# An attention and expert block: turned halves and split weights carried into the shared tiles; first rows loaded beside the constants, stacks cleared behind the first rows

## The chip, the cores and the metric

The kernel runs on one core of one Trainium2 chip. The core has a matrix engine (TensorE, PE in the rows), VectorE (DVE), ScalarE (ACT), GpSimd (POOL) and SyncE (SP), which here only issues DMA transfers. Each engine works through its own instructions in order and waits on semaphores that others raise. The metric is the time of one execution in microseconds (us); lower is better.

## The reference, cut to what matters

Two layers run over 8 sequences of 512 tokens of width 256, 4096 tokens in all.

```python
qkv = einsum('bsd,hde->bhse', x, Wqkv) + bqkv          # layer 0 attention, 16 heads of 16, causal
x = x + softmax(q @ k.T / 4) @ v @ Wout + bout         # with a layer norm before it
h = silu((xf @ w1 + b1) * (xf @ w3 + b3))              # layer 0 experts: 352 hidden units
y = sum over the 2 chosen of 8 experts of rw * (h @ w2 + b2)
z = shared expert, same form, on every token           # y + z is added to x
...                                                    # layer 1: gated scan, latent experts
```

Products in f32 are made of three products in f16: each operand is split into a high half and a low half (value minus high half), and high x high, low x high and high x low are summed.

## The kernel before, in words

Three phases follow each other, each a block that ends with a barrier over all engines.

**Mix phase** (`mix_phase`): for each sequence b the normalised rows xn are turned (transposed) on PE, split by ACT (`x_high`) and DVE (`x_low`) into `xT_hi` and `xT_lo`, and give q, k, v and the router's logits. q and k go through DRAM into `q_stack` and `k_stack` (`store_hi`, `load_stacks` on SP). The heads follow, three steps a head (`at = 3*head + n`), and the preparation of the next sequences hangs on these steps by tables (`AT_X_T`, `AT_Q`, ...). xn is also stored to DRAM, as rows. A small block before it, `constants`, makes identity matrices on POOL while the others wait. The mix block begins with nine loads on SP, a clearing of `q_stack` on DVE and one of `k_stack` on POOL. It ends when SP has seen the last store of x1 (the residual) land.

**Experts phase** (`experts_phase`): tiles of 256 tokens. The shared expert takes 16 of them: tiles 0 to 10 first (`HEAD` and, the last two, `TURN`), then the routed tiles, 8 experts with at least two tiles each, then the last five shared ones (stages 0 to 4). A tile is, on PE: `gate_up` for m = 0 and 1, the four transposes that turn the rows of the next tile (`x_transposes`), `gate_up` for m = 2, then `out` of the tile before. Each `gate_up` is 12 products of 256 columns, `out` is 18. ACT and DVE split the turned rows (`x_part`), add biases, gate (`prod`), apply silu (`h`, `h_hi`, `h_lo`) and sum the output (`y`). `gate_up` of a tile waits for the `prod` of the tile before. In the first tiles DVE also does `place`, which writes one-hot columns (`in_column`), 7 a tile, and a split of later weights (`pack_lo`); POOL writes 64 one-hot rows (`in_lane`), then 8 columns and 2 more. After tile 8 PE multiplies all of them (`table`) into the list of tokens that POOL then gathers by.

Before tile 0 the phase loads the shared expert's weights and the first rows, turns the rows and splits both; `find_slots` on DVE works out the slots from the router's results, and only then can DVE do anything for tile 0.

**Layer 1** (`layer1_phase`) begins when the last shared tile is done; its first normalisation hangs on gathered rows that DVE adds in stages 2 and 3.

## Time and profile before

| what | us |
|---|---|
| three runs: lowest, median, highest | 1232.79, 1236.97, 1238.09 |
| the profiled execution | 1237.58 |
| its span, first to last instruction | 1235.8 |
| PE busy | 1124.0 |
| DVE busy | 914.1 |
| ACT busy | 682.2 |
| POOL busy | 529.9 |

The shares are averages over phases: the mix phase takes the first 463 us, the experts phase runs to about 845, layer 1 to the end. Where two rows of one engine stand back to back, a change matters if it removes one of them; where a row shows idle time with a releaser, the releaser sets the time.

### The profile page before, as it was taken

The numbers are of one execution on the slowest core, as the hardware profiler recorded it, in microseconds if no ns is written. First come the engines' busy times: TensorE is split into PE (matmuls) and PEld (weight loads), VectorE is DVE, ScalarE is ACT, GpSimd is POOL, SyncE is SP. The second block draws the span as 40 slices with busy tenths as digits, with TensorE's granted clock in tenths as the row PEclk, the third lists the DMA queues.
The fourth block names the chain that finished last, engine by engine and source line by source line (L and its number), as shares of the span: only waits on it lengthen the run. The fifth ranks groups of instructions, "written<-read, shape, count | busy, mean of one in ns | idle before, by whom it ended". The sixth has DMA issues, their size and how long they took to land. (4 is left out here: it accounts for less than half of the span.)

```text
span 1235.8 us, 26934 instructions
## 1 busy us (share of the span) xinstructions
PE 1124.0 (91%) x8964; PEld 751.5 (61%) x8965; DVE 914.1 (74%) x2224; ACT 682.2 (55%) x1478; POOL 529.9 (43%) x751
## 2 busy tenths in 40 slices
PE   4789999999999966998999999997999999999998
PEld 2345555555555435887999888883555555546555
DVE  4778898888887826885756667674877977977866
ACT  2256565665556544665656666655554654664553
POOL 5343333424333228833444443332635546447314
PEclk9689999999999997999999999998999999999999
DMA  4437524445234106656232453442231241332302
GB/s 137 82 72 215 108 45 95 95 78 102 45 79 87 18 35 190 192 161 197 76 126 81 123 163 122 121 141 69 81 126 41 97 129 42 102 94 72 107 8 97
DMA packets 98276, 125.17 MB, mean 101 GB/s; under 512 B 14480, under 2 KB 87888, under 8 KB 97168
## 3 DMA queue, kind: packets, MB, share of 16 engines
q1 hardware_dynamic: 87184, 105.07, 31.9%
q0 software_dynamic: 6912, 18.88, 5.5%
q8 instruction: 47, 0.77, 0.3%
q10 hardware_dynamic: 4096, 0.14, 0.2%
q14 instruction: 37, 0.30, 0.1%
HBM read 84.70 MB, written 39.19 MB: 100 GB/s over the span
## 5 line engine op out<-in xcount | busy, mean ns | idle before, releaser
L479 ACT ACTIVATE p<-bank 128x384 f32<-128x384 f32 (+1 forms) x384 | 191.5, 530 | 186.0 <-PE bank L855 119.6
L688 DVE TENSOR_REDUCE neg_max<-bank 128x1 f16<-128x384 f32 (+3 forms) x352 | 219.6, 640 | 65.0 <-PE bank L843 62.2
L397 POOL TENSOR_SCALAR_AFFINE_SELECT p<-p 128x256 f32<-128x256 f32 x256 | 103.6, 409 | 245.4 <-ACT p L479 244.7
L121 PE MATMUL xbank<-gT_hi,w_hi 128*128 128x256 f16 (+1 forms) x636 | 175.0, 275 | 15.3 <-DVE w_lo L1448 6.0
L122 PE MATMUL xbank<-gT_lo,w_hi 128*128 128x256 f16 (+1 forms) x636 | 174.7, 275 | 0.0
L123 PE MATMUL xbank<-gT_hi,w_lo 128*128 128x256 f16 (+1 forms) x636 | 174.6, 274 | 0.0
L840 PE MATMUL bank<-k_stack,q_stack 96*128 96x384 f16 (+3 forms) x512 | 133.5, 313 | 20.1 <-DVE neg_max L688 12.6
L1382 ACT ACTIVATE a<-xbank,b 128x256 f32<-128x256 f32 x159 | 74.3, 468 | 65.9 <-PE xbank L123 62.4
L1293 POOL DMA_INDIRECT fetched<-xn_dram,token_now x80 | 81.4, 1017 | 42.9 <-POOL token_now L1289 30.7
L1934 POOL TENSOR_TENSOR up_lo<-up_sq,up_hi 128x512 f16<-128x512 f32 x32 | 43.2, 1378 | 126.6 <-ACT up_hi L1991 126.6
L1467 DVE SCALAR_TENSOR_TENSOR prod<-xbank,b,a 128x256 f32<-128x256 f32 x159 | 73.8, 476 | 31.4 <-ACT a L1382 23.7
L855 PE MATMUL bank<-q_stack,k_stack 97*128 97x512 f16 (+1 forms) x256 | 91.1, 360 | 3.8 <-ACT p L479 3.8
L1945 POOL TENSOR_TENSOR he_lo<-he_sq,he_hi 128x512 f16<-128x512 f32 x64 | 75.6, 1200 | 43.4 <-ACT he_hi L2032 43.4
L121 PE MATMUL xbank<-w_hi,h_hi 128*128 128x256 f16 (+1 forms) x318 | 88.1, 277 | 5.4 <-DVE y L1482 5.4
L843 PE MATMUL bank<-mask_qk,identb 128*128 128x128 bf16 (+2 forms) x352 | 89.1, 253 | 0.0
L122 PE MATMUL xbank<-w_lo,h_hi 128*128 128x256 f16 (+1 forms) x318 | 87.9, 277 | 0.0
L123 PE MATMUL xbank<-w_hi,h_lo 128*128 128x256 f16 (+1 forms) x318 | 87.9, 276 | 0.0
L2032 ACT ACTIVATE he_hi<-he_sq 128x512 f16<-128x512 f32 x64 | 39.4, 627 | 85.0 <-DVE he_sq L2169 85.0
L873 PE MATMUL bank<-p,v_aug 128*32 128x512 f32 (+3 forms) x1024 | 83.1, 443 | 0.8 <-DVE o_rows L668 0.8
L1473 DVE TENSOR_TENSOR h_lo<-h,h_hi 128x256 f16<-128x256 f32 x159 | 66.9, 425 | 22.6 <-ACT h_hi L1391 21.9
L121 PEld LDWEIGHTS xbank<-gT_hi,w_hi 128*128 128x128 f16 (+1 forms) x636 | 67.9, 107 | 25.1 <-issue 12.1
L840 PEld LDWEIGHTS bank<-k_stack,q_stack 96*128 96x128 f16 x512 | 45.0, 99 | 59.0 <-DVE neg_max L688 41.1
(304 smaller groups left out, 3065.5 us busy)
## 6 DMA issues: line engine op xcount, KB each, us to landing
w_bc<-wT_dram SPq DMA_DIRECT2D x8, 2048.0 KB, 8.3
y_routed_dram<-y SPq DMA_DIRECT2D x37, 256.0 KB, 2.1
w<-in_w SPq DMA_DIRECT2D x11, 704.0 KB, 6.8
pack<-in_pack SPq DMA_DIRECT2D x12, 342.0 KB, 4.0
xr<-in_x SPq DMA_DIRECT2D x8, 512.0 KB, 7.3
xn_dram<-xn SPq DMA_DIRECT2D x8, 512.0 KB, 3.1
qk_hi_dram<-qk_hi SPq DMA_DIRECT2D x16, 256.0 KB, 2.8
qk_lo_dram<-qk_lo SPq DMA_DIRECT2D x16, 256.0 KB, 2.6
```

Of the source, the lines that this page charges most:

```text
L121: pe.matmul(out, hi_a(c), hi_b(c), start=first and x == 0, stop=False)
L122: pe.matmul(out, hi_a(c), lo_b(c), start=False, stop=False)
L123: mm = pe.matmul(out, lo_a(c), hi_b(c), start=False, stop=last and x == n - 1)
L397: pool.affine_select(out=diagonal, in_=diagonal, pattern=[[0, 2], [1, P]], compare_op=ALU.is_ge, fill=0.0, base=0, channel_multiplier=-1). ...
L479: act.activation(p32[:, s // GH % 2, s % GH, cols], s_bank[n][:, 0:cols.stop - cols.start], ACT.Exp).then_inc(p_exp.sem, 1)
L688: dve.tensor_reduce(neg_max[:, g % 2, 0:GH * TT].rearrange("p (h t) -> p h t", t=TT)[:, heads[0]:heads[-1] + 1, j], a_bank[c % 2][:, 0:len ...
L840: pe.matmul(to[:, at * w:(at + 1) * w], q_stack[0:STK, u, h0 + h, j * P:(j + 1) * P], k_stack[0:STK, u, h0 + h, 0:w], start=at == 0, stop= ...
L843: pe.matmul(diagonal, identb[:, :], mask_qk[:, 0:len(heads), :], start=False, stop=True).then_inc(a_psum.sem, 1)
L855: mm = pe.matmul(to[:, 0:S - n * P], k_stack[0:AUG, u, h, n * P:(n + 1) * P], q_stack[0:AUG, u, h, n * P:S], start=True, stop=True)
L873: mm = pe.matmul(out_bank[VW * h:VW * (h + 1), k * P:S], v_aug[:, b % 2, k, GH * (g % NG) + h, :], p32[:, g % 2, h, P_OFF[k]:P_OFF[k] + S ...
L1293: pool.indirect_dma_start(fetched[:, u, half, :], None, dram["xn"], bass.IndirectOffsetOnAxis(token_now[:, u, half:half + 1], 0)).then_inc ...
L1945: pool.tensor_tensor(he_lo[:, e, :], he_sq[:, e % EB, :], he_hi[:, e, :], ALU.subtract).then_inc(he_lo_s.sem, 1)
```

## The change

1. **First loads.** The loads of x for sequence 0 and of wqkv are issued by SP inside the `constants` block. The clearing of `q_stack` and of `k_stack` moves behind the work on the first rows.
2. **Turned halves.** In the mix phase SP stores `xT_hi` and `xT_lo` of every sequence to DRAM (`store_xT`, 2 x 256 KB each). The shared tiles, all but tile 11 (stage 0), load them ready split into one of two `turned` tiles; their transposes and `x_part` go away. Tile 11 and the routed tiles keep theirs.
3. **Split weights.** The shared expert's weights are loaded and split in the last sequence of the mix phase, into tiles that outlive it (`Carried`). Biases come from there too. The loads of expert 1's and 2's weights move by a tile or two.
4. **Barrier.** The mix block no longer waits for the last store of x1; the load that needs it does.
5. **Columns.** DVE places 8 columns in each of tiles 0 to 7 (64 in all), POOL none of these.

```diff
-AHEAD = 2
-PLACED_BY_DVE = 56
-PLACED_A_TILE = 7
+PLACED_BY_DVE = 64
+PLACED_A_TILE = 8
+AT_SHARED = (3, 5, 8, 10)
+class Carried:
...
+        self.first = sb("shared_in", [P, 2 * DC * 3 * D], F16)
+        self.second = sb("shared_out", [P, 2 * len(HT) * D], F16)
+        self.turned = sb("turned", [P, 2, 2, DC, ETOK], F16)
+        self.bias = sb("shared_b13", [P, 2 * len(HT)])
...
 # mix phase, SP
-            sp.dma_start(xr[:, :, :], rows(x, 0)).then_inc(x_loaded.sem, 16)
-            sp.dma_start(wqkv32[:, :, :], w["wqkv"].rearrange("(c p) n -> p c n", p=P)).then_inc(wqkv_loaded.sem, 16)
...
+            def store_xT(b):
+                sp.wait_ge(xT_lo_s.sem, xT_lo_s.at(b))
+                for k, of in enumerate((xT_hi, xT_lo)):
+                    sp.dma_start(dram["xnT"][b][:, k], of[:, :, :]).then_inc(xT_stored.sem, 16)
...
             store_xn(0)
             load_x(1)
+            store_xT(0)
...
+                if b + 1 == NB:
+                    sp.wait_ge(xT_stored.sem, xT_stored.at(0))
+                    load_shared()
...
-            sp.wait_ge(x1_stored.sem, x1_stored.at(NB - 1))
+            sp.wait_ge(x1_stored.sem, x1_stored.at(NB - 2))
+            sp.wait_ge(xT_stored.sem, xT_stored.at(NB - 1))
 # mix phase, POOL
-            clear(k_stack, 0)
...
             inverse_std(0)
+            clear(k_stack, 0)
 # mix phase, ACT (and the like on DVE, two steps later, into the low halves)
+            def split_shared(n):
...
+                if n < 2:
+                    act.activation(carried.w13_hi[:, n, :], w13_32[n], ACT.Copy).then_inc(w_hi.sem, 1)
+                elif n == 2:
+                    act.activation(carried.w2_hi[:, 0:2, :], w2_32[:, 0:2, :], ACT.Copy).then_inc(w_hi.sem, 1)
...
+                    elif at - 28 in AT_SHARED:
+                        split_shared(AT_SHARED.index(at - 28))
 # constants
+        @block.sync
+        def _(sp):
+            sp.dma_start(carried.xr[:, :, :], w["x"][0:S, :].rearrange("(t p) d -> p t d", p=P)).then_inc(carried.x_loaded.sem, 16)
+            sp.dma_start(carried.wqkv32, w["wqkv"].rearrange("(c p) n -> p c n", p=P)).then_inc(carried.wqkv_loaded.sem, 16)
 # experts phase, SP
+            def load_turned(n, tile, read):
+
+                sp.wait_ge(gu_psum.sem, gu_psum.at(read))
+                sp.dma_start(turned[:, n % 2], turned_tile(dram["xnT"], tile)).then_inc(turned_loaded[n % 2].sem, 16)
...
-                if stage == HEAD:
-                    load_x(i + AHEAD)
                 load_pack(i)
+                load_turned(i + 2, i + 2 + (i + 2) // HEAD_TILES, i)
...
             def prologue():
-                load_x(0)
-                load_weights(0, 0)
                 load_biases(0, 0)
-                load_x(1)
 # experts phase, ACT (the same on DVE, after find_slots)
             def prologue():
                 act.activation(identh[:, :], identf[:, :], ACT.Copy).then_inc(identh_s.sem, 1)
-                x_part(0)
-                for c in range(DC):
-                    split_in(0, 0, c, 0)
-                split_out(0, 0, 0)
...
-                if has_next(stage):
+                if next_routed(i, stage):
                     x_part(i + 1)
 # experts phase, PE
-                pe.wait_ge(gT_lo_s.sem, gT_lo_s.at(i))
-                gate_up(i, u, 0)
-                gate_up(i, u, 1)
-                if has_next(stage):
-                    x_transposes(i + 1, stage == HEAD or is_int(i, HEAD_TILES - AHEAD), stage + 1 if stage in range(TAIL_TILES) else 0)
-                gate_up(i, u, 2)
+                n = shared_place(i, stage)
+                if n is None:
+                    pe.wait_ge(gT_lo_s.sem, gT_lo_s.at(i - HEAD_TILES))
+                else:
+                    pe.wait_ge(turned_loaded[n % 2].sem, turned_loaded[n % 2].at(n // 2))
+                gate_up(i, u, 0, n)
+                gate_up(i, u, 1, n)
+                if next_routed(i, stage):
+                    x_transposes(i + 1)
+                gate_up(i, u, 2, n)
```

DVE at the start of the mix phase, before (line numbers are the source's; xr holds the rows of x, xn the normalised ones):

```order
L535 UNCONDITIONAL_BRANCH [waits barrier_Pool_Activation_PE_DVE_SP_release]
L539 MEMSET q_stack 96x4096
L542 MEMSET route_run 128x8
L543 MEMSET neg_max 128x32
L549 BN_STATS stats<-xr 128x6 [waits x_loaded,cleared]
```

And of the change, from the split of the gate's weights to the low halves of k:

```order
L784 TENSOR_SCALAR bq<-bqk 128x2 [waits w_loaded]
L786 TENSOR_TENSOR gate_lo<-gate,gate_hi 128x16 [waits w_hi]
L788 TENSOR_TENSOR wout_lo<-shared_out,wout_hi 128x512 [waits w_hi]
L608 MEMSET q_stack 96x4096
L646 SCALAR_TENSOR_TENSOR qk_lo<-bank,bqk,qk_hi 128x512 [waits qk_hi_s] x2
```

The clearing of `q_stack` moved from ahead of the first statistics to ahead of the first low half of k.

PE where the experts phase begins, before (xg holds a tile's rows, gT_hi and gT_lo the turned halves, w_hi and w_lo the weights' halves):

```order
L1624 UNCONDITIONAL_BRANCH [waits barrier_Pool_Activation_PE_DVE_SP_release]
L1636 MATMUL xbank<-identf,xg 128x128 [waits tile_loaded]
L1636 MATMUL xbank<-identf,xg 128x128 x3
L121 MATMUL xbank<-gT_hi,w_hi 128x256 [waits e_lo,prod_s,gT_lo_s]
L122 MATMUL xbank<-gT_lo,w_hi 128x256
```

And of the change (the weights' halves stand in shared_in):

```order
L1695 UNCONDITIONAL_BRANCH [waits barrier_Pool_Activation_PE_DVE_SP_release]
L149 MATMUL xbank<-turned,shared_in 128x256 [waits prod_s,turned_loaded0]
L150 MATMUL xbank<-turned,shared_in 128x256
L151 MATMUL xbank<-turned,shared_in 128x256
L149 MATMUL xbank<-turned,shared_in 128x256
```

The first product follows the barrier with no transposes, no load and no split in between.

DVE from the end of `find_slots` through tile 0 to tile 1, of the change:

```order
L1675 CAST lanes_half<-lanes 128x128 [waits slots]
L1614 COPY slot<-pos 128x8
L1615 COPY wk<-route_weights 128x8
L1541 SCALAR_TENSOR_TENSOR prod<-xbank,shared_b,a 128x256 [waits h_hi_s,a1_s,b_loaded]
L1541 SCALAR_TENSOR_TENSOR prod<-xbank,shared_b,a 128x256 [waits h_hi_s,a1_s]
L1541 SCALAR_TENSOR_TENSOR prod<-xbank,shared_b,a 96x256 [waits h_hi_s,a1_s]
L1547 TENSOR_TENSOR h_lo<-h,h_hi 128x256 [waits h_hi_s] x2
L1547 TENSOR_TENSOR h_lo<-h,h_hi 96x256 [waits h_hi_s]
L1609 TENSOR_SCALAR in_column<-lanes_half,pos_f,ids 128x114 [waits lanes_half_s]
L1609 TENSOR_SCALAR in_column<-lanes_half,pos_f,ids 128x114 x7
```

Before, five rows stood between the copy of `wk` and the first `prod`: one `gT_lo` and four splits of weights; `find_slots` itself has not moved.

## Rows read from the trace of the kernel before

**Rows 1.** Windows, a shared tile's stretch: PE, PEld, DVE, ACT, POOL busy, clock, DMA
```profile
507.10:513.46 6.36, 6.36 (x61) 5.87 (x60) 6.09 (x18) 4.29 (x11) 6.36 (x9) 1.00 0.59 182
```

**Rows 2.** Timeline, the start: start, us, engine, line, operation, idle before
```profile
0.79 0.53 POOL L981 MEMSET zeros<- 128x512 f32 x1 [0.29 <-POOLq L2436]
...
2.54 0.65 POOL L996 TENSOR_SCALAR_AFFINE_SELECT mask_qk<-zeros 128x512 bf16<-128x512 f32 x1
...
3.66 0.45 SPq L274 DMA_DIRECT2D xr<-in_x  x1
...
4.59 3.47 DVE L539 MEMSET q_stack<- 96x4096 f32 x1 [4.46 <-PEq L972]
...
8.15 1.41 DVE L549 BATCH_NORM_STATS2 stats<-xr 128x6 f32<-128x256 f32 x4
...
12.84 0.21 ACT L437 ACTIVATE gate_hi<-gate 128x16 f16<-128x16 f32 x1 [1.74 <-DMA shared_b_row<-in_b]
...
22.12 0.75 DVE L578 SCALAR_TENSOR_TENSOR qk_lo<-bank,bqk,qk_hi 128x512 f16<-128x512 f32 x1 [5.07 <-ACT qk_hi L461]
```

**Rows 3.** Timeline, ACT in the last sequence's heads
```profile
441.16 1.36 ACT L479 ACTIVATE p<-bank 128x512 f32<-128x512 f32 x3 [0.50 <-PE bank L855]
...
442.87 2.80 ACT L479 ACTIVATE p<-bank 128x512 f32<-128x512 f32 x6
```

**Rows 4.** Timeline, the end of the mix phase to tile 1
```profile
460.30 0.38 SPq L294 DMA_DIRECT2D x_dram<-x  x1
...
463.56 0.82 SPq L1220 DMA_DIRECT2D xg<-xn_dram  x2
...
469.35 0.16 DVE L1540 COPY wk<-route_weights 128x8 f32<-128x8 f32 x1
...
470.28 1.47 ACT L1363 ACTIVATE w_hi<-w 128x704 f16<-128x704 f32 x2 [2.43 <-DMA w<-in_w]
...
473.24 0.37 PE L121 MATMUL xbank<-gT_hi,w_hi 128*128 128x256 f16 x1 [6.01 <-DVE w_lo L1448]
...
481.67 0.28 PE L121 MATMUL xbank<-gT_hi,w_hi 128*128 128x256 f16 x1 [1.48 <-DVE gT_lo L1460]
```

**Rows 5.** Windows, the first products of tile 0
```profile
473.00:476.00 3.00, 2.76 (x14) 1.98 (x15) 1.01 (x2) 0.00 (x0) 3.00 (x5) 0.50 0.00 0
```

**Rows 6.** Timeline, PE: one tile's transposes and the product behind
```profile
490.66 0.60 PE L1636 MATMUL xbank<-identf,xg 128*128 128x128 f32 x4
...
491.10 0.27 PE L121 MATMUL xbank<-gT_hi,w_hi 128*96 128x256 f16 x1
```

**Rows 7.** Timeline, PE: transposes of later tiles
```profile
499.42 0.66 PE L1636 MATMUL xbank<-identf,xg 128*128 128x128 f32 x4 [2.25 <-DMA xg<-xn_dram]
...
512.14 0.60 PE L1636 MATMUL xbank<-identf,xg 128*128 128x128 f32 x4
518.48 0.60 PE L1636 MATMUL xbank<-identf,xg 128*128 128x128 f32 x4
```

**Rows 8.** Timeline, DVE in a shared tile
```profile
505.31 1.76 DVE L1534 TENSOR_SCALAR in_column<-lanes_half,pos_f,ids 128x114 f16<-128x114 f16 x7
...
508.54 0.67 DVE L1460 TENSOR_TENSOR gT_lo<-xbank,gT_hi 128x512 f16<-128x512 f32 x1
```

**Rows 9.** Tile in_lane: ns min/median/max, first and last start
```profile
L1320 POOL TENSOR_SCALAR in_lane<-lanes,pos_f x64: 592/604/1713, 469.3 to 512.2; 128x128 f16<-128x128 f32 x64
```

**Rows 10.** Timeline, POOL's last column and PE's table
```profile
519.68 2.32 POOL L1328 TENSOR_SCALAR in_column<-lanes,tail_at,tail_ids 128x114 f16<-128x114 f32 x2
...
535.01 3.48 PE L1699 MATMUL xbank<-in_column,in_lane 128*128 128x114 f16 x64
```

**Rows 11.** Tile xg: landing of a tile's rows after issue
```profile
DMA to landing us min/median/max: 2.0/3.1/6.1
```

**Rows 12.** Timeline, the last shared tiles
```profile
808.47 0.28 PE L121 MATMUL xbank<-gT_hi,w_hi 128*128 128x256 f16 x1 [1.05 <-DVE gT_lo L1460]
...
829.58 0.99 DVE L1549 SCALAR_TENSOR_TENSOR x<-rows_k,wk,x 128x256 f32<-128x256 f32 x2
```

More of the change, by code:

```diff
@@ L341, in _ @@
                 if b + 1 < NB:
+                    store_xT(b + 1)
                     store_hi(b + 1, 0)
@@ L494, in out_copy @@
                 act.activation(o_cols[:, g % 2, :], out_bank[:, :], ACT.Copy).then_inc(o_copied.sem, 1)
+            def split_shared(n):
+                loads = shared_in_loaded if n < 2 else shared_out_loaded
+                act.wait_ge(loads.sem, loads.at(0))
+                if n < 2:
[3 more added lines that the diff above has]
+                else:
+                    act.activation(carried.w2_hi[0:HT[2][1], 2, :], w2_32[0:HT[2][1], 2, :], ACT.Copy).then_inc(w_hi.sem, 1)
             for c in range(DC):
@@ L1106, in experts_phase @@
         rows_moved = sig("rows_moved", 1)
-        x_loaded = sig("tile_loaded", 16 * HALF)
-        tail_loaded = [sig(f"tail_loaded{t}", 16) for t in range(1, TAIL_TILES)]
+        turned, turned_loaded = carried.turned, carried.turned_loaded
         gT_psum = sig("gT_psum", 1)
@@ L1142, in over_experts @@
             tile(1, 0, 0, HEAD)
-            for i in range(2, HEAD_TILES - AHEAD):
+            for i in range(2, HEAD_TILES - 2):
                 tile(i, 0, 0, HEAD)
@@ L1258, in tile @@
                     load_pack(PACK_PARTS - 1)
-                    for t in range(1, TAIL_TILES):
-                        rows = dram["xn"][(HEAD_TILES + t) * ETOK:(HEAD_TILES + t + 1) * ETOK, :]
-                        sp.dma_start(tail_rows[:, t - 1, :, :], rows.rearrange("(h p) d -> p h d", p=P)).then_inc(tail_loaded[t - 1].sem, 16)
             def last(e, u, first):
@@ L1321, in _ @@
             ins.then_inc(lane_placed.sem, 1)
-            for t in range(PLACED_BY_DVE // 2, T // P):
-                for k in range(2):
-                    ins = pool.tensor_scalar(in_column[:, 2 * t + k, :], lanes[:, 0:columns], pos_f[:, 0, t, k:k + 1],
-                                             ids[:, t:t + 1], ALU.is_equal, ALU.mult)
-            ins.then_inc(column_placed.sem, 1)
             for k in range(TAIL_PLACES):
@@ L1604, in prologue @@
                 find_slots()
-                x_part(0)
-                for c in range(DC):
-                    split_in(0, 0, c, 0)
-                split_out(0, 0, 0)
             def after_first(e, u, first):
@@ L1636, in x_transposes, with gate_up @@
                         mm = pe.transpose(bank[3][:, c * ETOK + half * P:c * ETOK + half * P + P],
-                                          rows[:, half, c * P:(c + 1) * P], identf[:, :])
+                                          xg[:, half, c * P:(c + 1) * P], identf[:, :])
                 mm.then_inc(gT_psum.sem, 1)
-            def gate_up(i, u, m):
+            def gate_up(i, u, m, n):
                 h0, M = HT[m]
+                x_hi, x_lo = (xT_hi, xT_lo) if n is None else (turned[:, n % 2, 0], turned[:, n % 2, 1])
                 pe.wait_ge(prod_s.sem, prod_s.at(i - 1, m + 1))
@@ L1705, in after_first @@
                 if not is_int(e, 0):
-                    pe.wait_ge(e_lo.sem, e_lo.at(e))
+                    pe.wait_ge(e_lo.sem, e_lo.at(e - 1))
                     pe.nop(nofuse=True)
-            over_experts(pe, lambda: x_transposes(0, True), new_expert, tile, after_first, lambda e, u, first: None, table, out)
+            over_experts(pe, lambda: None, new_expert, tile, after_first, lambda e, u, first: None, table, out)
 PACK = {}
```

208 lines of the change are left out of this document (126 added, 82 removed).

## The prediction

> **What bounds the kernel now.** I read the windows first, then the timeline at each place that the diff touches, then single tiles. In a shared tile PE has no gap, 6.36 us of 6.36, and DVE is busy for 6.09 of them, POOL for all; the clock is 1.00, its 2.4 GHz level [rows 1]. So PE bounds these tiles and DVE stands close behind. Two tiles' transposes stand 6.34 apart (512.14 and 518.48), which is the period of a tile [rows 7]. Between the phases nothing bounds but a chain: x1 is stored at 460.30, the next phase's first load is issued at 463.56, weights arrive for ACT at 470.28, the first product starts at 473.24 after 6.01 idle, and tile 1 at 481.67 [rows 4]. That chain is where most of the change acts.
>
> **1. Start.** x is issued at 3.66, and its statistics start at 8.15, right behind a clearing of `q_stack` that runs from 4.59 to 8.06 [rows 2]. So x had landed within 4.5 us of its issue at the latest. SP will now issue it where the first operation of `constants` stands, at about 0.8 [rows 2]: landed by 5.3, and DVE is free from about 4.8. The gain is 2.85 to 3.35, say 3.1. The last of the nine small loads reaches ACT at 12.84 [rows 2]; ACT must split the gate's and the output's weights from it before the turned rows. It was issued at about 7.7, 5.1 earlier. Now it is the eighth behind two that went ahead, issued at 7.2, and takes between 2.0, the shortest landing of a tile's rows [rows 11], and the same 5.1. ACT then turns to the rows at 10.0 to 13.1, where everything else is ready at 11.0 (14.1 less 3.1). The middle, 11.6, gives 2.5 of gain. Against it, `store_xT(0)` puts 512 KB between the next x and the stores of q and k, all on one queue: 0 to 1.4, I take 0.5. The moved clearing (3.47 us) is hidden: DVE had 5.07 idle before the first low half of k at 22.12 [rows 2], which now comes near 19.6, and the clearing starts near 14. The one on POOL (as long, estimated) falls into POOL's wait for the turned rows. If that cover were gone it would cost the overhang. **Start: -2.0 (-3.4 to -0.5).**
>
> **2. Mix phase.** Seven more pairs of stores go to SP between waits that end later anyway (q and k are products of the very halves that are stored), so nothing queues behind them. In the last sequence ACT gets four splits. Two of 704 columns took 1.47 together [rows 4]; the two for w2 (768 columns) are estimated from it at 0.9: 2.4 in all. There ACT runs its exponentials with little room: 0.50 idle before 441.16, then 2.80 in one piece [rows 3]. At most 2.4 - 0.5 = 1.9 reaches the end of the phase, at least nothing (PE has work of its own between). I take 1.0. DVE, which mirrors the splits, has no maxima left by then. **+1.0 (0 to +1.9).**
>
> **3. Between the phases.** The landing of x1 is no longer waited for. What is left is the issue (460.30 + 0.38) and a barrier; the one after `constants` took 0.47 (POOL's end at 3.19, first issue at 3.66) [rows 2, 4]. The phase begins at about 461.2 instead of 463.56. The `turned` halves and weights are there, so PE does tile 0 (36 products, about 3.9 us by 0.109 each) at once. Then it waits: `find_slots` ends 5.95 after the phase's first issue (469.51 less 463.56) [rows 4], and it has not moved. So DVE is free at 467.15, the first `prod` takes some 0.45, and tile 1 starts at 467.6 instead of 481.67. **DVE is late next**; behind `find_slots` are queued `prod`, the low halves and the columns, and PE waits for them. Before, tile 0 ran at clock 0.50, the 1.2 GHz level, after 6.01 idle [rows 4, 5]; the pause is now about 2 us, and I take full clock.
>
> **4. Shared tiles 1 to 8.** Four transposes cost 491.10 - 490.66 = 0.44 [rows 6]. A tile is then 6.34 - 0.44 = 5.90. DVE loses `gT_lo` and gains a column: seven take 1.76, one 0.25, and `gT_lo` takes 0.60 of its queue (0.67 less overlap) [rows 8]: 6.09 - 0.60 + 0.25 = 5.74, just under. The wait of 2.25 for a tile's rows [rows 7] goes. The table can start at 467.6 + 8 x 5.90 = 514.8. It also needs POOL. POOL starts `in_lane` at 469.3, 5.74 after the phase's first issue, and now at 466.95. Its 64 rows took 43.5 (469.3 to 512.2 and one more), against 64 x 0.604 = 38.7 by the median; the longest took 1.713 [rows 9]. Five bursts of DVE's columns lay in that time, so a burst of seven cost POOL 0.96. Eight bursts of eight cost 8.8: 466.95 + 38.7 + 8.8 = 514.4, and two columns of at least 0.8 make 516.0. Some of the excess may have other causes, so I take 515.5. Before, POOL ended at 522.0 and PE began at 535.01 [rows 10]: the 13 us of cover are gone. **Places 3 and 4 together: 535.0 - 515.5 = -19.5 (-20.2 to -17.5).**
>
> The Trainium skill (SBUF — State Buffer, Who interferes with whom) speaks against this: VectorE and GpSimd share a port pair as an "exclusive lock", and a 16-bit `tensor_scalar` can hold it for its whole length. By that rule every column stops POOL fully. The trace bears it out by half: a burst of 1.76 cost 0.96.
>
> **5. Tile 9** loses its transposes, tile 10 keeps them for tile 11: **-0.44**. The gather of the first routed rows shifts with the table.
>
> **6. Last shared tiles.** Stage 1 started at 808.47, after 1.05 idle for `gT_lo` [rows 12]. It will wait for `prod` instead, which DVE does just before. Stages 0 to 3 lose 0.44 each: at most 1.05 + 1.76 = 2.8. But layer 1 hangs on gathered rows that DVE adds from 829.58 [rows 12], and POOL's gathers start only when the last routed tile's y has landed, which moves by `gT_lo` alone, 0.6. I take 2.0. **-2.0 (-2.8 to -0.6).**
>
> **Sum.** -2.0 + 1.0 - 19.5 - 0.44 - 2.0 = -22.9. The profiled execution took 1237.58, which is 0.6 above the median of the three runs; so 1214.6 in its terms, 1214.0 beside the median. The routed tiles and layer 1 have the same work as before.
>
> **Rivals.**
> - *POOL is locked out in full.* DVE's eight bursts of 8 x 0.25 all add to POOL's 38.7: 466.95 + 38.7 + 16.1 + 1.2 = 523. The table waits 7.5 longer than forecast: 1221.5. For it: POOL's 1.713 us row. Against it: five bursts would have made 47.5 where 43.5 stood [rows 9]. 12 in 100. (That is the skill's rule of the exclusive lock taken whole.)
> - *Start and splits pay nothing back.* The small loads land as late as before and the ACT splits reach PE in full, the tail gives 0.6: -0.5 + 1.9 - 19.5 - 0.44 - 0.6 = -19.1, 1218. For it: the exponentials' solid 2.80 [rows 3]. 17 in 100.
> - *More than forecast.* Every term at its good end: -26.8, 1210; 6 in 100.
> - *The change doesn't do what it says*: the clock stays at its lower level through tile 0 and 1 (1.4 + 5.9 lost), and DVE bounds the tiles at 6.3, 3 more: 1224 to 1232. Against it: the short pause. 5 in 100.
> - *Slower.* The `turned` loads come late. One can be issued when tile i has done its `gate_up`, 3.9 into it, and is needed 11.8 after the tile's start: 7.9 of room. xg took 3.1 at the median and 6.1 at most [rows 11]. Thirteen loads must each be 1.8 over the room to eat 22.9, which means 9.7 to land; at 10.0 the time is 1214 + 13 x 2.1 = 1241. The pieces are half as long (512 bytes), which speaks for slower landing, but not threefold. 2 in 100.
> - The forecast (1210.5 to 1217.5): 58 in 100.
>
> **The numbers.** 1214.0. The range 1209 to 1222 takes in the first three rivals nearly whole, some 85 in 100 with the scatter of runs. A measurement of this kernel can tell about 0.5%, 6.2 us, from no change. All but the last two cases lie below 1230.8: faster 0.94, same 0.04, slower 0.02.
>
> **What would show it.** In the changed profile: statistics of x at about 5; PE's first product of the experts phase near 460 (461.2 less the start and split terms) at clock 1.00; one idle stretch of about 2.5 behind it, released by `prod`; then tiles 5.90 apart with no transposes; the table near 514.5 (515.5 less the same), released by POOL or by nothing; POOL's last column within 2 us of it. Wrong would be: tiles over 6.1 apart, waits for `turned` halves, a table released by POOL after 518, a mix phase longer than before by over 2, or a clock of 0.50 behind the barrier.

## The result

The changed kernel takes 1229.54 us (median of 8 runs, 1227.47 to 1233.48), the kernel before 1236.84 (8 runs, 1231.95 to 1243.53): ratio 0.9948, 95% interval 0.9925 to 0.997. Run again beside other kernels it took 1229.95, ratio 0.9946 (0.9923 to 0.9969). It is faster, by 7 us or 0.5%, which is clear of the scatter; forecast were 23, and a range of 1209 to 1222. The profiled execution took 1229.52, its span 1227.8, against 1237.58 and 1235.8 before.

The rows that answer to those of before follow in the order of the prediction's steps. **Start** (timeline of the changed kernel; start, us, engine, line, operation, idle before and what ended it):

```profile
4.64 1.41 DVE L617 BATCH_NORM_STATS2 stats<-xr 128x6 f32<-128x256 f32 x4 [0.78 <-DMA xr<-in_x]
8.08 4.48 DVE L635 TENSOR_SCALAR xn<-xr,mv,rstd 128x256 f32<-128x256 f32 x4 [1.56 <-issue]
...
7.93 3.51 POOL L427 MEMSET k_stack<- 96x4096 f32 x1
...
20.16 0.51 SPq L326 DMA_DIRECT2D xnT_dram<-xT_hi  x1
20.71 0.43 SPq L326 DMA_DIRECT2D xnT_dram<-xT_lo  x1
...
26.68 0.33 SPq L376 DMA_DIRECT2D q_stack<-qk_hi_dram  x1
...
32.12 0.58 PE L921 MATMUL bank<-k_stack,q_stack 96*128 96x128 f16 x4 [4.93 <-DMA k_stack<-qk_hi_dram]
```

The statistics start at 4.64, 3.5 earlier than in [rows 2]; forecast were 2.85 to 3.35. Then everything is given back: the normalising takes 4.48 us (1.38 before) just while POOL clears `k_stack`, so that it ends 0.35 earlier than before (12.56 for 12.91), and two more stores stand in front of q and k. The first product of scores comes at 32.12; before it came at 30.71.

**Phase border** (timelines of SP and PE, then windows with PE, PEld, DVE, ACT, POOL busy, clock, DMA share, GB/s):

```profile
462.80 0.37 SPq L345 DMA_DIRECT2D x_dram<-x  x1
463.76 0.36 SPq L1275 DMA_DIRECT2D b<-in_b  x1
...
464.10 0.27 PE L149 MATMUL xbank<-turned,shared_in 128*128 128x256 f16 x1 [2.13 <-PEq L161]
470.25 0.27 PE L149 MATMUL xbank<-turned,shared_in 128*128 128x256 f16 x1 [0.40 <-DVE prod L1541]
477.06 0.27 PE L149 MATMUL xbank<-turned,shared_in 128*128 128x256 f16 x1 [0.75 <-DVE prod L1541]
...
483.62 0.27 PE L149 MATMUL xbank<-turned,shared_in 128*128 128x256 f16 x1 [0.50 <-DVE prod L1541]
494.79 0.40 PE L149 MATMUL xbank<-turned,shared_in 128*128 128x256 f16 x1 [5.11 <-DMA turned<-xnT_dram]
...
527.13 3.47 PE L1769 MATMUL xbank<-in_column,in_lane 128*128 128x114 f16 x64 [0.56 <-DVE prod L1541]
```

```profile
462.00:464.00 2.00, 0.00 (x0) 0.00 (x0) 0.69 (x1) 0.22 (x1) 0.22 (x2) 1.00 0.13 46
464.00:466.00 2.00, 1.90 (x14) 1.55 (x15) 1.27 (x7) 0.09 (x1) 0.52 (x8) 0.76 0.89 266
466.00:468.00 2.00, 2.00 (x11) 1.45 (x10) 1.84 (x6) 0.47 (x1) 0.00 (x0) 0.50 0.88 255
...
492.00:494.00 2.00, 0.00 (x0) 0.00 (x0) 0.41 (x1) 0.00 (x0) 2.00 (x4) 0.59 0.43 140
494.00:496.00 2.00, 1.21 (x6) 0.89 (x7) 0.44 (x2) 0.77 (x1) 2.00 (x5) 0.50 0.56 101
```

x1's last store is issued at 462.80, 2.5 later than in [rows 4]; the border takes 0.96 (forecast 0.9), PE is at work 0.34 behind it, and tile 1 starts 6.49 after the phase's first issue (forecast 6.4). But the clock falls to its 1.2 GHz level in tile 0 (0.50 from 465.0 to 468.5). Tile 2 starts 6.81 after tile 1, tile 3 another 6.56 later, both released by `prod`, and then tile 4 waits 5.11 for its turned halves and starts at half clock.

SP, in front of that wait (timeline):

```profile
474.37 0.53 SPq L1308 DMA_DIRECT2D turned<-xnT_dram  x1
480.12 0.40 SPq L1312 DMA_DIRECT2D y_dram<-y  x1
...
481.61 0.91 SPq L1281 DMA_DIRECT2D b<-in_b  x2
482.56 0.44 SPq L1269 DMA_DIRECT2D w<-in_w  x1
...
483.56 2.20 SPq L1271 DMA_DIRECT2D w<-in_w  x1
485.80 0.63 SPq L1318 DMA_DIRECT2D pack<-in_pack  x1
486.47 0.68 SPq L1308 DMA_DIRECT2D turned<-xnT_dram  x1
```

Tile 2 had done its `gate_up` near 481 (477.06 + 3.9). The buffer was free then; the load that fills it is issued at 486.47, behind y(0) and the whole of expert 1. It lands 8.3 us later, the longest of the 13 in this phase (median 4.2; xg had 3.1 and at most 6.1, [rows 11]).

DVE in the same tiles and in a later one (timeline), the window of one round, then POOL's rows (the tile's line with ns min/median/max, and single rows from the timelines: two of the changed kernel, one of the kernel before):

```profile
483.00 1.25 DVE L1541 SCALAR_TENSOR_TENSOR prod<-xbank,shared_b,a 128x256 f32<-128x256 f32 x3
...
485.49 0.42 DVE L1547 TENSOR_TENSOR h_lo<-h,h_hi 96x256 f16<-96x256 f32 x1 [0.17 <-ACT h_hi L1468]
485.83 0.74 DVE L1556 TENSOR_TENSOR y<-xbank,xr 128x256 f32<-128x256 f32 x2
486.49 2.33 DVE L1609 TENSOR_SCALAR in_column<-lanes_half,pos_f,ids 128x114 f16<-128x114 f16 x8
488.72 0.86 DVE L1602 TENSOR_TENSOR pack_lo<-pack,pack_hi 128x684 f16<-128x684 f32 x1
489.50 1.26 DVE L1541 SCALAR_TENSOR_TENSOR prod<-xbank,shared_b,a 128x256 f32<-128x256 f32 x3
...
517.17 1.84 DVE L1609 TENSOR_SCALAR in_column<-lanes_half,pos_f,ids 128x114 f16<-128x114 f16 x8
```

```profile
483.00:489.50 6.50, 6.00 (x56) 5.34 (x54) 6.20 (x18) 3.87 (x10) 6.50 (x11) 1.00 0.76 202
```

```profile
L1402 POOL TENSOR_SCALAR in_lane<-lanes,pos_f x64: 590/596/1652, 469.5 to 509.2; 128x128 f16<-128x128 f32 x64
...
487.02 0.59 POOL L1402 TENSOR_SCALAR in_lane<-lanes,pos_f 128x128 f16<-128x128 f32 x1
488.75 1.30 POOL L1402 TENSOR_SCALAR in_lane<-lanes,pos_f 128x128 f16<-128x128 f32 x1
...
497.65 1.66 POOL L1320 TENSOR_SCALAR in_lane<-lanes,pos_f 128x128 f16<-128x128 f32 x1
```

While POOL works, one round of DVE is 6.50 (483.00 to 489.50) with no idle but 0.17 and 6.20 of it busy: DVE bounds. Eight columns take 2.33 there and 1.84 once POOL is done. POOL's 64 rows take 40.3 in all. The row at 487.02, beside columns, takes 0.59; the one at 488.75, beside `pack_lo`, takes 1.30. Rows follow each other 0.58 apart otherwise, which makes 37.1 for 64. Of the other 3.2, 3.0 stand in four places beside `pack_lo` and 0.2 beside columns.

The last shared tiles (timelines of SP and PE, windows):

```profile
806.97 0.38 SPq L1312 DMA_DIRECT2D y_dram<-y  x1
...
808.01 0.59 SPq L1308 DMA_DIRECT2D turned<-xnT_dram  x1
...
798.31 0.28 PE L149 MATMUL xbank<-turned,w_hi 128*128 128x256 f16 x1 [0.46 <-DVE prod L1541]
...
812.85 0.28 PE L149 MATMUL xbank<-turned,w_hi 128*128 128x256 f16 x1 [2.05 <-DMA turned<-xnT_dram]
```

```profile
815.00:820.00 5.00, 5.00 (x41) 4.29 (x40) 1.90 (x5) 2.05 (x5) 0.95 (x1) 0.84 0.53 175
```

Stage 1 starts at 798.31 instead of 808.47 [rows 12]; its buffer is free at 802.2, and the next load is issued at 808.01, behind the store of stage 0. Stage 3 waits 2.05 and runs in part at the lower clock.

### The profile page after: what moved, and what is told of

Its sections match the earlier page's. It is cut to its first block and busy times, and to the rows that moved or that the text cites. A ratio compares the mean times of both kernels' runs of the same rounds, so it can differ in the third digit from the quotient of the medians.

```text
span 1227.8 us, 26691 instructions
## 1 busy us (share of the span) xinstructions
PE 1118.7 (91%) x8873; PEld 747.1 (61%) x8905; DVE 915.4 (75%) x2217; ACT 676.3 (55%) x1463; POOL 520.6 (42%) x743
## 5 line engine op out<-in xcount | busy, mean ns | idle before, releaser
L1459 ACT ACTIVATE a<-xbank,b 128x256 f32<-128x256 f32 (+1 forms) x126 | 58.7, 469 | 55.1 <-PE xbank L151 51.5
L149 PE MATMUL ybank<-l_xT_hi,pack_hi 128*128 128x512 f16 x208 | 79.4, 382 | 0.9 <-DVE lat_lo L2251 0.7
L151 PE MATMUL ybank<-l_xT_hi,pack_lo 128*128 128x512 f16 x208 | 79.4, 382 | 0.0
L150 PE MATMUL ybank<-l_xT_lo,pack_hi 128*128 128x512 f16 x208 | 79.3, 381 | 0.0
L1541 DVE SCALAR_TENSOR_TENSOR prod<-xbank,b,a 128x256 f32<-128x256 f32 (+1 forms) x126 | 58.6, 477 | 25.9 <-ACT a L1459 22.9
L924 PE MATMUL bank<-mask_qk,identb 128*128 128x128 bf16 (+1 forms) x321 | 76.9, 240 | 0.0
L1466 ACT ACTIVATE h<-prod 128x256 f32<-128x256 f32 x159 | 64.9, 408 | 20.7 <-DVE prod L1541 13.5
L151 PE MATMUL ybank<-pack_hi,up_lo 128*128 128x256 f16 x256 | 69.8, 273 | 0.0
L150 PE MATMUL ybank<-pack_lo,up_hi 128*128 128x256 f16 x256 | 69.8, 273 | 0.0
L149 PE MATMUL ybank<-pack_hi,up_hi 128*128 128x256 f16 x256 | 69.8, 272 | 0.0
```

What stands on the lines that cost most here:

```text
L149: pe.matmul(out, hi_a(c), hi_b(c), start=first and x == 0, stop=False)
L150: pe.matmul(out, hi_a(c), lo_b(c), start=False, stop=False)
L151: mm = pe.matmul(out, lo_a(c), hi_b(c), start=False, stop=last and x == n - 1)
L924: pe.matmul(diagonal, identb[:, :], mask_qk[:, 0:len(heads), :], start=False, stop=True).then_inc(a_psum.sem, 1)
```

## The experiments

Each is the changed kernel with one edit, unless said otherwise. The expectations stand as they were recorded. Below them, a table with the readings of every profile.

**Weights behind turned halves.** SP, in `tile`:

```diff
                 load_turned(i + 2, i + 2 + (i + 2) // HEAD_TILES, i)
+                if is_int(i, 1): ... load_biases(1, 1); load_weights(1, 1)
+                if is_int(i, 3): ... load_weights(2, 0)
                 if before is not None:
                     store(i - 1, dram["y"], i - 1)
...
-                if is_int(i, 1): ...
-                if is_int(i, 3): ...
```

> The changed kernel with one move on SP's queue: in a shared tile the loads of expert 1 (tile 1) and expert 2 (tile 3) are issued right behind that tile's load of turned halves, ahead of the store of y, instead of behind it. Theory A (order in SP's queue): tile 4 waited 5.1 us because its halves were issued at 486.5, behind the store of y(0) at 480.1 and 5.2 us of issues for expert 1; now they are issued near 481 and tile 4 does not wait, the clock stays at 1.00 from tile 1 on, tiles stand 6.5 apart while POOL still works (DVE's columns at 0.30 each) and 5.92 after it, the table starts at 521.4 instead of 527.1, and the whole takes 1223.8 instead of 1229.5. Rival B (the transfers): the halves share the DMA engines with 1.1 MB of weights, so some tile between 2 and 5 still waits 3 us or more for its halves; table at 525 or later, whole 1227.5 or more.

Measured 1224.8 us. No tile up to the table waits for halves, and the table starts 59.16 after the phase's first issue instead of 63.37: 4.2 less, of 5.7 expected. Most of that goes with the clock, which stayed at 1.00 here in tile 0: two profiles below that have the changed kernel's order of loads and that clock start the table at 60.27 and 60.32, so the order by itself is worth 1.1 in these profiles. What it saves at tile 4 came back as a wait, in DVE's timeline:

```profile
487.50 0.76 DVE L1556 TENSOR_TENSOR y<-xbank,xr 128x256 f32<-128x256 f32 x2 [2.77 <-DMA y_dram<-y]
```

The store of y(0), now issued behind the weights, landed only there. So A holds for the halves, and B in a form of its own: what stands behind 1.1 MB pays.

**Last tiles' halves first.**

```diff
-                    if 1 <= stage and stage + 2 < TAIL_TILES:
-                        load_turned(HEAD_TILES + stage + 1, HEAD_TILES + stage + 2, i)
+                    if stage + 3 < TAIL_TILES:
+                        load_turned(HEAD_TILES + stage + 2, HEAD_TILES + stage + 3, i + 1)
                     store(i, dram["y"], HEAD_TILES + stage)
```

> The changed kernel with one move in the last shared tiles: the halves of stage s+3 are loaded as soon as stage s+1 has done its first products, ahead of the store of stage s. Theory A (order in SP's queue): the load for stage 3 was issued at 808.0 though its buffer was free at 802.2; now it is issued there, the wait of 2.05 us at 812.85 and the stretch at half clock behind it (about 2 us) go, and the end of the experts phase (first issue of layer 1, 838.6) comes 3 to 4 us earlier: 1226. Rival B: the end of the phase hangs on the gathered rows of the routed tiles and on DVE, so under 1 us comes back: 1229.

1224.96 us. No wait for halves, clock 1.00 up to 830.6 (28.6 into these tiles; in the changed kernel it falls at 813.2, 14.9 into them), and 36.87 from stage 1 to the phase's end where the changed kernel has 40.31. A holds.

**Clearing behind the normalising.**

```diff
             inverse_std(0)
+            pool.wait_ge(xn_ready.sem, xn_ready.at(0))
             clear(k_stack, 0)
```

> The changed kernel with POOL's clearing of k_stack made to wait until DVE has normalised the first rows. Theory A (DVE and POOL share a way to the buffer): the four normalising operations take 1.4 us instead of 4.48 and end at 9.5 instead of 12.56; ACT's first turned rows still wait for the small loads (gate_hi at 11.9) and come at 12.65 instead of 13.76: 1.1 us at the start. The next operation of DVE beside the clearing, wqkv_lo (1.75 us), may be stretched in turn. Whole 1228.4 instead of 1229.5. Rival B: the normalising is slow for another reason (late rows or a late reciprocal): it stays at 4.5 us.

1224.45 us. Its timeline:

```profile
8.28 1.38 DVE L636 TENSOR_SCALAR xn<-xr,mv,rstd 128x256 f32<-128x256 f32 x4 [1.56 <-issue]
9.57 1.75 DVE L781 TENSOR_TENSOR wqkv_lo<-shared_in,wqkv_hi 128x1536 f16<-128x1536 f32 x1
...
9.72 3.51 POOL L427 MEMSET k_stack<- 96x4096 f32 x1 [1.54 <-DVE xn L636]
```

The normalising is back at 1.38, so A holds. The same clearing does nothing to the subtraction beside it (1.75, as before). The gain at the first scores is 2.0 (30.18), more than the 1.1 expected: the first turned rows come 1.6 earlier (12.14 for 13.76), and PE's products for q and k stand 0.43 apart until 17.1 here and until 21.2 in the changed kernel, and 0.22 apart behind that, though the granted clock reads 1.00 throughout. What ends the slow stretch is open.

**Without the splits.** (`elif at - 28 in AT_SHARED: split_shared(...)` and its like on DVE removed, two memsets on POOL. It leaves out the shared expert's weights and computes with zeros.)

> The changed kernel without the splitting of the shared weights on ACT and DVE in the last sequence (left out: the shared expert is computed from zeros that POOL writes; loads as before). Theory A (ACT is on the path there): the changed kernel lost 1.4 us before 436 and 1.1 us more between 436 and the last store of x1 (462.80); without the splits that store comes at 461.7, and the whole takes 1228.4. Rival B (the splits are free and the lateness is all from the start): the last store stays at 462.8 within 0.2.

1225.56 us. From the output copy near 434 to the last store of x1: 26.36, exactly that of the kernel before, so the 1.1 of this stretch is the splits'. A holds for it. The store itself comes at 460.36, not 461.7: the part from the first scores to that copy is 1.5 shorter than in the changed kernel, which the edit does not touch. Over all profiles that part scatters between 401.4 and 404.2.

**Splits early.** `AT_SHARED = (3, 5, 8, 10)` becomes `(-6, -3, 0, 3)`.

> The changed kernel with the four splits of the shared weights moved from steps 31, 33, 36 and 38 of the last sequence to steps 22, 25, 28 and 31, where ACT still has idle time between its exponentials (2.5 to 3.6 us busy of every 5). Measured so far: from the output copy near 434 to the last store of x1 the kernel before takes 26.36 us, the one without splits 26.36, and the four profiles with splits 27.47, 28.83, 30.71 and 30.73. Theory A (the splits stand in ACT's solid stretch, and PE behind it sometimes falls to half clock): this stretch is 26.4 to 27 again, and the time from the first product of scores to the last store of x1 is 428 to 430.5; whole 1.1 to 4 us less than the changed kernel. Rival B (2.75 us of ACT work is paid wherever it stands): first scores to last store stays at 431 or more.

1224.94 us; 26.44 for the stretch, 428.65 from first scores to last store. The copy ahead of the stretch comes 13.55 behind the one before it, where the kernel before has 12.93: the splits now cost 0.6 there. A holds in this profile; of the four later ones with the same places one has 26.44 again and three have 28.02 to 29.69.

**Turned rows stored later.**

```diff
-            store_xT(0)
             for half in range(2):
                 store_hi(0, half)
                 load_stacks(0, half)
+                if half == 0:
+                    store_xT(0)
```

> The changed kernel with the two stores of the first batch's turned rows (512 KB) issued behind the first half's stacks instead of in front of the stores of q and k. Theory A (the low half of q and k lands late because it queues behind them): the first load into the stacks is issued at about 25.3 instead of 26.7 and the first product of scores comes at 30.7 instead of 32.1 to 32.3 (four profiles): whole 1.4 us less. Rival B (the landing is slow for the sake of the next x load, which was there before, too): first scores at 32 again.

1225.52 us; the first load into the stacks is issued at 25.23, and the first scores come at 30.86. A holds: 1.3.

**Columns 7 and 8, with the weights moved.** `PLACED_BY_DVE = 56`, `PLACED_A_TILE = 7`, and POOL's eight columns as before.

> The kernel with the expert weights issued behind the turned halves, and in it the columns dealt as in the kernel before: seven a tile by DVE (56) and eight by POOL. In the run with the weights moved, DVE was busy without a gap in tiles 3 to 6, which stood 6.50 apart (prod 1.25, low halves 1.65, y 0.74, eight columns 2.32, pack 0.86), and the table started 59.16 after the phase's first issue. Theory A (DVE bounds these tiles): with seven columns they stand 6.2 apart, POOL ends its work about 6 us later (at 54 to 56 after the phase's first issue, still before the table), and the table starts at 57.5. Rival B (PE or the transfers bound, or POOL's eight columns now release the table): 59 or more.

1223.34 us. DVE's rounds behind tile 3 are 6.14, 6.27, 6.15 and 6.06 (`prod` at 491.67, 497.81, 504.08, 510.23, 516.29), as forecast, and POOL ends at 55.83. The table starts at 58.46, not 57.5: this profile had the low clock in tile 0, the one with the weights moved had not, and DVE waited 1.74 for a store of y. A holds for the period.

**The changed kernel again.**

> The changed kernel itself once more, beside the others on the same chip, for how far its parts scatter. Every theory: first product of scores at 32.1 to 32.3; from the output copy near 435 to the last store of x1 between 27.4 and 30.8; table 62.5 to 63.5 after the phase's first issue; idle of 3.6 to 5.2 us for turned halves at tile 4 and about 2 us in the last shared tiles; from the first product of the last four shared tiles to the end of the phase 38.5 to 41.3.

1229.95 us. Two readings lie just outside what was written, the table at 62.37 and the wait at tile 4 of 3.42; the others lie within.

The kernels with one edit up to here, and the one with two, have medians between 1223.34 and 1225.56, whatever the edit. That is 4 to 7 below the changed kernel, but does not tell them from each other, and it is more than some edits can account for (the last but one gains 1.3 at the first scores and 4.4 in the median). So the readings of the profiles carry the argument, and not the medians.

**Weights spread over tiles 2 to 5**, on top of the kernel with columns 7 and 8:

```diff
+                if i in (2, 3): load_weights(1, 1, i - 2)   # part 0: w13, part 1: w2
...
+                if i in (4, 5): load_weights(2, 0, i - 4)
```

> The last kernel (expert weights behind the turned halves, columns 7 and 8) with the weights of experts 1 and 2 spread: biases in tile 1, the first product's weights in tile 2, the second's in tile 3, and so on to tile 5. In both runs with all of expert 1 in one tile, the store of that tile's y landed only after 7 us and DVE waited 2.8 us for it before the next y. Theory A (the bytes ahead of it on the queue): that wait falls to under 1 us and the table starts 56.5 to 57.5 after the phase's first issue (58.46 and 59.16 before). Rival B (the wait is shifted to a later tile): 58.4 again.

The group of four kernels that this one belongs to ran where layer 1 took 415 to 418 us instead of 389 to 391.5, in each of them; so its times (1254.71 here, 1269.92 for the kernel before) count as ratios only: 0.9869 (0.9851 to 0.9888). y's wait is gone, but the table starts at 58.18 all the same, because something else is late next:

```profile
523.75 5.03 PE L1781 MATMUL xbank<-in_column,in_lane 128*128 128x114 f16 x64 [2.83 <-POOL in_column L1416]
```

POOL's columns, which ended 2.6 ahead of the table in the run before, now release it. They end 2.1 later after the phase's first issue than there (57.93 for 55.83), because POOL's 64 rows take 43.5 for 41.1; the largest part of what they take beyond 0.58 each stands beside `pack_lo` in both. Neither theory had that.

**Idle products at the border.**

```diff
                 out_products(NB - 1, g, last_out[g])
+            for n in range(12):
+                pe.matmul(s_bank[0][:, 0:D], wout_hi[:, 0, 0:P], wout_hi[:, 0, :], start=True, stop=True)
```

> The changed kernel with twelve idle products of 256 columns (1.3 us, into a free bank) behind PE's last products of the first phase, so that it rests about 1 us at the phase border instead of 2.13. Theory A (the low clock in tile 0 is not free): five profiles fell to clock 0.50 within tile 0 and had the table 62.4 to 63.5 after the phase's first issue, the one with early splits kept 1.00 and had 60.27 with the same order of loads. So here the clock stays at 1.00 through tile 0, the store of y(0) is issued at about 14.6 instead of 16.4 after the phase's first issue, and the table starts at 60.3 to 61. Rival B (find_slots on DVE ends when the slow tile 0 does, so the clock costs nothing): 62.4 or more.

Ratio 0.9914 (0.9889 to 0.994). Its timeline of PE:

```profile
463.84 0.27 PE L149 MATMUL xbank<-turned,shared_in 128*128 128x256 f16 x1 [0.82 <-PEq L161]
469.99 0.27 PE L149 MATMUL xbank<-turned,shared_in 128*128 128x256 f16 x1 [2.06 <-DVE prod L1543]
```

Clock 1.00 in tile 0, the forecast's idle stretch of 2.06 released by `prod`, tile 1 at the same distance from the phase's first issue (6.48), and the table at 60.32. A holds: though `find_slots` hides the slow tile 0 itself, the store of y(0) is 1.6 late (16.35 after the phase's first issue for 14.73) and the table 2.1 to 3.2. (The expectation's "five profiles" are six in the table below, from 62.37 to 63.53.)

**All mends together**, twice, and two variants:

> All mends together: POOL's clearing behind the normalising, the first turned rows stored behind the first stacks, splits at steps 22 to 31, weights of the experts behind the turned halves and spread, columns 56 and 8, and the loads of the last shared tiles ahead of the stores. Theory A (each loss found so far is separate and on the path): against the changed kernel 3.4 us at the start, 1.1 to 4.4 in the last sequence, 2 by the clock in tile 0, 6 before the table and 3.3 in the last shared tiles: about 15 us, so 1215 (ratio to the kernel before 0.983). Rival B (they overlap, and the routed tiles or DMA take them back): 1220 or more.

> All mends together and the twelve idle products ahead of the phase border. Theory A (with the early splits the clock mostly holds already): within 1 us of the kernel without the idle products, 1215. Rival B (the clock falls there in most executions even with early splits): 2 us less than without them.

> All mends together, once more. Theory A (the stalls of PE in the last shared tiles belonged to that session): no wait for turned halves there, 36.9 to 37.5 us from the first product of the last four shared tiles to the phase's end, and about 1213 where the kernel before takes 1237 (ratio 0.981). Rival B (the stalls belong to this kernel's code and come again): 40.5 or more there, and 1216.

> All mends but that of the last shared tiles, whose loads are issued behind the stores as in the changed kernel. Theory A (the order of SP's queue is paid there): waits of 2 to 3 us for turned halves at the third of these tiles, 39.5 to 41 us to the phase's end, and 2 to 3 us more in the whole than with the mend. Rival B (something else takes it back): the same time as with the mend within 1 us.

All mends: ratio 0.9823 (0.9804 to 0.9842), and the second time 1217.44 us, 0.9866 (0.9837 to 0.9895). The first meets the forecast of 0.983, the second misses the 0.981 that was written for it. With idle products 0.9851 (0.9829 to 0.9874): no gain from them, and 3.6 us more between the medians, which neither theory has. Without the mend of the last tiles 1222.23 us, 0.9895 (0.9878 to 0.9913), on the same chip as the 1217.44, with a wait of 2.28 for halves in stage 3: A holds. That order of SP's queue is worth 3.6 us in the profiles (40.53 for 36.95) and 4.8 between the medians, with intervals that overlap. In the first profile with all mends PE was idle in stage 3 with nothing to wait for:

```profile
805.42 0.31 PE L149 MATMUL xbank<-turned,w_hi 128*96 128x256 f16 x1 [0.42 <-issue]
...
808.29 0.27 PE L151 MATMUL xbank<-turned,w_lo 128*96 128x256 f16 x1 [1.12 <-issue]
```

The kernel with idle products, in the same group of runs, has such gaps at the same place (0.77, 0.86, 0.46 and 0.45 from 809.33 on). In the second profile of all mends, on another chip, there are none and the stage-1-to-end reading is 36.95: so the kernel's code alone does not make them. What PE waited for there is open.

The readings. "Scores": start of the first product of scores. "Stretch": from the output copy near 434 to the issue of the last x1. "Clock": in the first 3 us of the new phase. "Table" and "last": the table's start after the phase's first issue, and from the first product of stage 1 to the phase's end.

| kernel | scores | stretch | clock | table | last | median, us |
|---|---|---|---|---|---|---|
| before | 30.71 | 26.36 | 0.67 | 71.45 | 37.10 | 1236.84 |
| changed | 32.12 | 27.47 | 0.71 | 63.37 | 40.31 | 1229.54 |
| changed again | 32.21 | 27.47 | 0.65 | 62.37 | 40.74 | 1229.95 |
| weights moved | 32.34 | 28.83 | 1.00 | 59.16 | 39.67 | 1224.80 |
| last tiles | 32.23 | 30.71 | 0.61 | 62.55 | 36.87 | 1224.96 |
| clearing | 30.18 | 30.73 | 0.63 | 62.52 | 38.50 | 1224.45 |
| no splits | 32.25 | 26.36 | 0.74 | 63.53 | 41.25 | 1225.56 |
| splits early | 32.30 | 26.44 | 1.00 | 60.27 | 41.10 | 1224.94 |
| rows later | 30.86 | 30.71 | 0.66 | 63.33 | 41.02 | 1225.52 |
| columns 7 and 8 | 32.07 | 30.74 | 0.61 | 58.46 | 39.26 | 1223.34 |
| spread | 32.26 | 28.59 | 0.76 | 58.18 | 40.29 | (0.9869) |
| idle products | 32.30 | 27.46 | 1.00 | 60.32 | 39.74 | (0.9914) |
| all | 29.30 | 28.10 | 0.61 | 57.45 | 40.74 | (0.9823) |
| all, idle products | 28.91 | 29.69 | 1.00 | 57.60 | 40.99 | (0.9851) |
| all again | 29.26 | 26.44 | 1.00 | 57.33 | 36.95 | 1217.44 |
| all but last tiles | 28.78 | 28.02 | 1.00 | 57.45 | 40.53 | 1222.23 |

The stretch comes in steps, and the granted clock tells them apart. Profiles with no fall to 0.50 in it have 27.46 or 27.47 with late splits (three of nine), 26.44 with early ones (two of five) and 26.36 with none. With one fall it is 28.59 and 28.83 late, 28.02 and 28.10 early; with two, 30.71 to 30.74 late (four profiles) and 29.69 early. So ACT's splits cost 1.1 in their late places, and each fall 1.1 to 2.1 more. Windows of the kernel with the last tiles mended (30.71) show the end of one fall in a stretch in which PE is busy throughout:

```profile
462.00:464.00 2.00, 2.00 (x11) 1.35 (x10) 0.00 (x0) 0.00 (x0) 0.00 (x0) 0.50 0.00 0
464.00:466.00 2.00, 2.00 (x14) 1.52 (x13) 0.69 (x1) 0.00 (x0) 0.00 (x0) 0.66 0.00 0
```

## Why the prediction was wrong

What the change removes was read rightly: no turning in the shared tiles, early first products, x1 no longer waited for. What waits in its place was not: the turned halves behind other work in SP's queue, DVE's round, and the clock. The table came 7.9 earlier, not 20.5. The profiled execution came out 14.9 above the forecast of 1214.6. By the prediction's steps:

1. **Start, -2.0: it was +1.4.** The step said that the clearing on POOL "falls into POOL's wait for the turned rows". It does, but it falls on DVE's normalising, too, and stops the first of its four operations for its whole length (3.51). The lost 3.1 are shown by the run that moves the clearing (2.0 back at the first scores). `store_xT(0)`, priced at 0.5 within 0 to 1.4, costs 1.3 (the run that moves it). The small loads took 4.9 (issued at 6.98, ACT at work at 11.88), near the bad end of the 2.0 to 5.1 that were taken for them; so with both mends the first scores are still only 1.5 earlier than before (29.26).
2. **Mix phase, +1.0: +1.1 in this profile,** right for ACT, and within its bounds. What the bounds left out is that PE's clock falls in this stretch in other profiles, up to 4.4 in all. That the splits cause the falls is not shown: they come in six of nine profiles with late splits and in three of five with early ones, and there is one profile without splits and one of the kernel before.
3. **Border and tile 1: right** to 0.1 each, counted from the last store (0.96 for 0.9, 6.49 for 6.4). "I take full clock" was wrong: nine of thirteen profiles of changed kernels without idle products fell to the lower level behind the same 2.13 of idle time. That costs 2.1 to 3.3 at the table (62.37 to 63.53 against 60.27 and 60.32, same loads and columns). It held in three of four profiles with early splits and in one of nine with late ones or none; why is open.
4. **Shared tiles: 47.9 forecast from tile 1 to the table, 56.9 measured.** This is the step that failed most. Counted from the phase's first issue the forecast is 54.3 and the changed kernel has 63.37; by single profiles, about 3.1 go with the clock (60.3 without its fall), 3.0 with the loads' order and the columns' share (57.3 to 57.6 with all mends), and the last 3.0 are there with all mends, too, where POOL places eight columns again and releases the table. Three terms of the step:
   - "One can be issued when tile i has done its `gate_up`": it can, but SP issues in order, and ahead of it stand y(0) and expert 1. 5.5 late, 8.3 to land, 5.11 of wait, and a restart at half clock: from tile 3's start to tile 4's are 11.17, 5.3 over 5.90, and the five tiles to the table take 2.8 over. The rival "turned loads come late" had the mechanism, but priced it as 13 equal delays by landing alone; it is one delay, by the queue. Moving the loads takes the wait away, but gives back 1.1 at the table and not 5.3, since the store of y(0) then lands late.
   - "5.74, just under" for DVE: its round is 6.50 while POOL works. The 5.74 was made of busy time, which measured 6.20: eight columns took 2.33, not 2.01 (1.76 for seven), the two first low halves 1.06 for 0.92 before. The 1.76 was one burst; the five of the kernel before that stand beside POOL's rows last 1.64 to 1.99. Of the other 0.30, 0.17 is a wait for ACT and the rest time between operations that no row counts as busy. Tiles 1 and 2 took 1.6 more than twice 5.90; the run with seven columns shows 6.2.
   - "So a burst of seven cost POOL 0.96": the excess was put down to the wrong operations of DVE. In the kernel before, rows also follow each other 0.58 apart otherwise, and of the 6.3 over 64 of these 2.7 stand beside `pack_lo` (the row at 497.65 with its 1.66 is one), 1.6 beside the split of the weights in tile 0 (the longest row, 1.713, is there), 1.4 beside low halves of h, and 0.4 beside columns. That is read from where the long rows lie; the changed kernel, without the split in tile 0, takes 40.3 for 43.5. POOL was free at 511.3, 16 before the table, and for the columns it is DVE that pays, 0.5 a burst. The Trainium skill (SBUF — State Buffer, Who interferes with whom) says that the loser of the port pair that VectorE and GpSimd share "fully blocks", by order of issue; the normalising beside the clearing agrees (4.48 for 1.38), the columns beside POOL's rows don't show it in either direction. The same section says that a DVE instruction with two inputs in the buffer contends with a POOL instruction that reads there and not with one that only writes. The subtraction beside the clearing agrees (1.75 both times), and so do POOL's rows, which read, beside `pack_lo` (1.30 and 1.66 for 0.59).
5. **Tile 9 and the routed tiles, -0.44: -2.3** from the table to stage 1 (271.18 for 273.46). The other profiles of changed kernels have 269.7 to 273.9 there, a scatter that is wider than the term; no run takes it apart.
6. **Last tiles, -2.0: +3.2.** "It will wait for `prod` instead" is true of stage 1. Stage 3 waits for its halves, again because of a store ahead in SP's queue. The run that turns the order round has 36.87, 3.4 less than the changed kernel.

3.6 (start and mix phase) + 0.1 + 9.0 (tiles) + 3.4 (behind the table) - 1.1 (layer 1, 389.18 for 390.23, within the 388.9 to 391.5 of the other profiles) make the 14.9. The rival "the change doesn't do what it says" has the measured time in its range, 1224 to 1232, but for other sums: it took the clock to fall through tiles 0 and 1 and DVE to bound all tiles at 6.3. DVE did bound, for 1.6 in tiles 1 and 2; the rest of the 14.9 it did not have, and that its number fits is luck. The mends of 1, 2, 4 and 6 together bring 1217.44 on one chip and a ratio of 0.9823 in the other group (1215 of 1237): most of what the forecast held for possible was there to be had. What now bounds the table is POOL, in the second profile of all mends:

```profile
517.47 3.48 PE L1783 MATMUL xbank<-in_column,in_lane 128*128 128x114 f16 x64 [2.52 <-POOL in_column L1418]
```

## What to carry to other kernels

When a load is made smaller or earlier, its room is counted from the moment at which its queue reaches it, not from the moment at which its buffer is free: read the issuing engine's rows in front of it, with each store that waits for a result and each large load between. A piece of work moved "into the idle time of its engine" needs a look at what the other engines do in that time as well. And once a bound falls away, work out the full round of the engine that stands 5% behind it, operation by operation: it is the next bound.

## What the runs showed of the hardware

- A clearing of 96x4096 on POOL (3.51 us) holds up the normalising of 128x256 f32 on DVE beside it (four take 4.48 instead of 1.38, the first alone 3.51), but not a subtraction of 128x1536 (1.75 with and without). Before, two such clearings ran side by side on DVE and POOL in 3.47 and 3.51.
- POOL's `tensor_scalar` of 128x128 (0.59 us) takes 1.30 to 1.66 beside DVE's subtraction of 128x684 from f32 to f16 (0.86 us), and 0.59 beside DVE's f16 columns of 128x114, which themselves go from 0.23 to 0.29 each.
- The clock in the first 3 us behind one and the same idle time of 2.13 us at the border is 1.00 in four profiles and falls below 0.77 in nine. With 0.82 of idle time it stayed at 1.00 in both profiles; in one of these it fell in tile 1, at 471.2.
- The first products for q and k (512 columns) stand 0.43 us apart until 20.7 in the kernel before, and 0.22 behind that, while the granted clock reads 1.00.
- One group of runs had layer 1 at 415 to 418 us where the others have 389 to 391.5, for all four kernels of the group, with the phases ahead unchanged.
